# A macaron block on one core: attention probabilities turned by a transposing DMA in place of TensorE transposes

## What is computed

```
x = x + 0.5 * ffn(layernorm(x), router_weight, w_in, w_out, bias)
x = x + attn(layernorm(x), w_q, w_k, w_v, w_o, b_o)
x = x + 0.5 * ffn(layernorm(x), router_weight, w_in, w_out, bias)
# attn: 16 heads of 16; softmax(mask(q k^T) / sqrt(256)) v, then w_o and b_o
# ffn: 8 experts, the best 2 of each token, silu(a) * b, hidden size 512
```

## Time and profile before

| what | value |
|---|---|
| median of 3 runs | 430.71 us (430.55 to 431.05) |
| the profiled execution | 430.32 us, of which the span is 428.6 us |
| TensorE busy | 402.1 us |
| VectorE, ScalarE, GpSimd busy | 299.3, 257.1, 249.2 us |
| mean granted clock of TensorE | 0.975 of 2.4 GHz |
| first mixture layer, attention, close, second layer | about 0 to 153, to 281, to 304, to 428.6 us |

### The profile page before, as it was taken

How to read it: one execution, slowest core, us unless ns; L and a number is a source line. 1 busy time by engine, 2 the same in 40 slices (tenths; PEclk the granted TensorE clock), 3 DMA queues, 4 the chain that set the end, 5 groups by cost and what they waited for, 6 DMA issues and landing times.

```text
span 428.6 us, 10138 instructions
## 1 busy us (share of the span) xinstructions
PE 402.1 (94%) x2892; PEld 331.2 (77%) x2893; DVE 299.3 (70%) x612; ACT 257.1 (60%) x640; POOL 249.2 (58%) x312
## 2 busy tenths in 40 slices
PE   7779999999999989799999999888899999999996
PEld 3558888888888767588888888674588888888884
DVE  6878997756655895877677676967356775566566
ACT  2737866565556455788788787722365555655552
POOL 5355457765478169577777677200555596654860
PEclk9889999999999999999999999966999999999999
DMA  7959911211111800000000000007641212112136
GB/s 253 400 143 397 363 55 40 66 44 61 55 46 38 271 32 2 1 3 3 2 0 0 0 0 0 2 1 254 208 153 50 61 40 66 57 49 55 43 99 219
DMA packets 22059, 38.90 MB, mean 91 GB/s; under 512 B 3217, under 2 KB 14737, under 8 KB 21777
## 3 DMA queue, kind: packets, MB, share of 16 engines
q1 hardware_dynamic: 17168, 24.41, 16.6%
q0 software_dynamic: 4576, 12.07, 9.4%
q10 hardware_dynamic: 288, 2.10, 1.3%
HBM read 29.37 MB, written 9.19 MB: 90 GB/s over the span
## 4 chain that ended last, share of the span: by engine, by line
PE 64%; DVE 15%; DMA 8%; issue 5%; ACT 3%; POOL 3%; ACTq 0%; SPq 0%; DVEq 0%; POOLq 0%
PE bank L1379 25%; PE bank L1401 12%; PE bank L1549 6%; PE bank L1389 4%; PE bank L1560 4%; DMA w_out<-y_scratch 3%; PE bank L1516 3%; PE bank L1355 2%; DMA unused_rows<-in_wr_t,own_row 2%; DMA arena<-xn_scratch,gather_row 1%; DVE arena L902 1%; DMA y_scratch<-arena,scatter_row 1%; DVE pT_lo L1185 1%; DVE v L1255 1%; PE bank L1550 1%
## 5 line engine op out<-in xcount | busy, mean ns | idle before, releaser
L533 POOL DMA_INDIRECT arena<-xn_scratch,gather_row x46 | 51.4, 1117 | 60.8 <-PE bank L1355 39.5
L539 POOL DMA_INDIRECT y_scratch<-arena,scatter_row x42 | 61.1, 1454 | 34.8 <-ACT arena L707 32.0
L1043 DVE TENSOR_TENSOR wo_lo<-w_out,wo_hi 128x1024 fp32r<-128x1024 f32 x46 | 61.2, 1330 | 4.1 <-PE bank L1401 2.5
L1379 PE MATMUL bank<-w_hi,xT_hi 128*128 x184 | 62.4, 421 | 0.0
L1048 DVE TENSOR_TENSOR gT_lo<-bank,gT_hi 128x512 fp32r<-128x512 f32 x46 | 31.7, 689 | 38.7 <-ACT gT_hi L681 38.7
L1379 PE MATMUL bank<-w_hi,xT_lo 128*128 x184 | 57.7, 394 | 0.0
L1379 PE MATMUL bank<-w_lo,xT_hi 128*128 x184 | 57.3, 392 | 0.0
L674 ACT ACTIVATE arena<-bank 128x512 f32<-128x512 f32 x46 | 27.5, 598 | 46.7 <-PE bank L1379 46.7
L619 POOL TENSOR_TENSOR k_head<-k_hi,head_mask 128x256 fp32r<-128x256 f32 x64 | 38.7, 625 | 28.1 <-PE bank L1550 21.0
L696 ACT ACTIVATE wo_hi<-w_out 128x1024 fp32r x46 | 48.8, 1061 | 5.5 <-issue 3.4
L1032 DVE TENSOR_TENSOR xT_lo<-bank,xT_hi 128x256 fp32r<-128x256 f32 x46 | 19.5, 424 | 35.8 <-ACT xT_hi L666 35.6
(11 more groups left out here) (197 smaller groups left out, 961.5 us busy)
## 6 DMA issues: line engine op xcount, KB each, us to landing
w_raw<-in_win_t SPq DMA_DIRECT2D x8, 1024.0 KB, 9.7
w_out<-in_wout_t SPq DMA_DIRECT2D x16, 512.0 KB, 7.8
w_out<-y_scratch SPq DMA_DIRECT2D x8, 512.0 KB, 6.2
xn_scratch<-arena ACTq DMA_DIRECT2D x2, 1024.0 KB, 6.0
x<-in_x SPq DMA_DIRECT2D x4, 256.0 KB, 3.7
out<-x SPq DMA_DIRECT2D x4, 256.0 KB, 2.1
arena<-xn_scratch,gather_row POOLq DMA_INDIRECT x46, 3.5
y_scratch<-arena,scatter_row POOLq DMA_INDIRECT x46, 3.0
```

The costliest lines, as they stand in the source:

```text
L533: pool.indirect_dma_start(out=xb[j % 2][:, :], out_offset=None, in_=xn_dram, in_offset=bass.IndirectOffsetOnAxis(ap=gather_row[:, j:j + 1] ...
L539: pool.indirect_dma_start(out=y_dram, in_=y[j % 2][:, :], in_offset=None, out_offset=bass.IndirectOffsetOnAxis(ap=scatter_row[:, j:j + 1], ...
L1043: dve.tensor_tensor(wo_lo[:, :, :], w_out[:, bass.ds(e, 1), :, :].rearrange("p o c d -> p (o c) d"), wo_hi[u][:, :, :].bitcast(F32), ALU.s ...
L1379: last = pe.matmul(bank[2 * half + u][:, :], tok[u][:, k, :], wts[:, bass.ds(e, 1), k, half * H:(half + 1) * H], start=(part == 0 and k == ...
```

## The change

Exponentials are written back in place, into the bank of the scores. `high` and `low` now come before the turn: they split these banks into `parts`, a f16 buffer of 2 x 6 x 128 columns per parity, in one instruction for the tail tiles (512 columns) and one for the head tiles (256). SP issues one transposing DMA per pair, `parts` to `pT` (32 in all); `weigh` reads `pT` and waits for the DMA. TensorE's `turn_probs` is gone. Head scores alternate between banks 2 and 3. The drain's and the close's warming matmuls, the place of the expert scores in `finish`, and the order on VectorE there change as well. The half bias is now added by VectorE, in four instructions per layer behind blocks 5 and 6. The rehearsal is gone; VectorE's first split of weights waits until GpSimd has issued the first gather.

```diff
-VBANK = (6, 4, 5, 3, 5, 6, 5, 6)
+VBANK = (3, 4, 5, 6, 5, 6, 5, 6)
-WARM_START, WARM_RANKS, WARM_PLAN, WARM_TURNED = 12, ((6, 5), (6, 5)), (6, 6), (4, 4)
-WARM_END, WARM_TURN2, WARM_CHOSEN = 2, 2, 2
+WARM_START, WARM_RANKS, WARM_PLAN, WARM_TURNED = 12, ((6, 5), (6, 5)), (10, 8), (4, 4)
+WARM_END = 6
-WARM_LN = (5, 1, 0, 0)
+WARM_LN = (5, 2, 1, 0)
+WARM_LAST = (4, 4)
+WARM_FINISH = (3, 2, 1)
...
+            def turn_parts(g):
+                u = g % 2
+                sp.wait_ge(low_ready, g * 2 + 2)
+                if g > 1:
+                    sp.wait_ge(pv_done, g * 2 - 2)
+                sp.dma_start(pT[u][:, :, :], parts[u][:, :, :, :].rearrange("p a t k -> p (a t k)"), transpose=True)\
+                    .then_inc(pT_ready[u], 16)
+
             for f in range(2):
                 if f:
+                    for g in range(BATCH * HPAIRS):
+                        turn_parts(g)
...
-            rehearse()
...
-                if f == 0:
-                    pool.wait_ge(rehearsed, 16)
...
                 for j in range(AHEAD):
                     gather(f, j)
+                    if f == 0 and j == 0:
+                        pool.sem_inc(first_begun)
...
-                    reach(act, probsT_done, g * 2 - 2)
                     for hh in range(2):
                         h = 2 * p + hh
-                        act.activation(probs[u][:, hh, 1:3, :],
-                                       bank[u][:, hh * SEQ:(hh + 1) * SEQ].rearrange("p (k t) -> p k t", k=2), ACT.Exp,
-                                       bias=neg_max[u][:, 1, hh:hh + 1],
+                        keys = bank[u][:, hh * SEQ:(hh + 1) * SEQ]
+                        act.activation(keys, keys, ACT.Exp, bias=neg_max[u][:, 1, hh:hh + 1],
...
             def high(b, s):
                 g = b * HPAIRS + (s - SLAG - 1)
-                for hh in range(2):
-                    act.wait_ge(probsT_done, g * 2 + (hh + 1))
-                    reach(act, pv_done, g * 2 + (hh - 3))
-                    act.activation(pT_hi[(s - 1) % 2 * 2 + hh][:, :, :],
-                                   bank[3 + hh][:, 0:3 * P].rearrange("p (k t) -> p k t", k=3),
-                                   ACT.Copy, scale=P_SCALE).then_inc(pT_hi_ready, 1)
+                u = (s - 1) % 2
+                reach(act, pT_ready[u], b * (16 * HPAIRS // 2) + (s - SLAG - 1) // 2 * 16)
+                act.wait_ge(tail_probs_ready, g * 2 + 2)
+                act.activation(parts[u][:, 0, 0:4, :], bank[u][:, :].rearrange("p (t k) -> p t k", t=4), ACT.Copy,
+                               scale=P_SCALE).then_inc(high_ready, 1)
...
+            def add_half_bias(f, i):
+                dve.wait_ge(bias_loaded, 32)
+                dve.wait_ge(xn_ready, TILES * 2 * f + 2 * i + 2)
+                two = x[:, 2 * i:2 * i + 2, :]
+                dve.scalar_tensor_tensor(two, bc(bias_row[:, :], 1, [P, 2, D]), 0.5, two, ALU.mult, ALU.add)\
+                    .then_inc(bias_added, 1)
...
                 if f == 0:
+                    dve.wait_ge(first_begun, 1)
                     split_low(0)
...
+            def low(b, s, tail):
+                g = b * HPAIRS + (s - SLAG - 1)
+                u = (s - 1) % 2
+                tiles = slice(0, 4) if tail else slice(4, 6)
+                source = bank[u][:, :] if tail else bank[2 + u][:, 0:2 * P]
+                dve.wait_ge(high_ready, g * 2 + (1 if tail else 2))
+                dve.scalar_tensor_tensor(parts[u][:, 1, tiles, :], source.rearrange("p (t k) -> p t k", k=P), P_SCALE,
+                                         parts[u][:, 0, tiles, :], ALU.mult, ALU.subtract).then_inc(low_ready, 1)
...
-                    reach(pe, tail_probs_ready, g * 2 - 2)
+                    reach(pe, low_ready, g * 2 - 3)
...
-                    reach(pe, head_probs_ready, g * 2)
-                    to = bank[2][:, 0:2 * P].rearrange("p (h k) -> p h k", h=2)
+                    reach(pe, low_ready, g * 2 - 2)
+                    to = bank[2 + u][:, 0:2 * P].rearrange("p (h k) -> p h k", h=2)
...
             def weigh(b, s):
+                turned = pT[(s - 1) % 2]
+                pe.wait_ge(pT_ready[(s - 1) % 2], b * (16 * HPAIRS // 2) + ((s - SLAG - 3) // 2 + 1) * 16)
...
                 turn_half(0)
-                score_experts(1, (1,))
+                warm(WARM_FINISH[0])
                 turn_half(1)
                 project_half(0)
                 project_half(1)
                 turn(2, (2,))
-                warm(WARM_TURN2)
+                score_experts(1, (1,))
```

More of the change, by code:

```diff
@@ L332, in build @@
         tail_probs_ready = sem("tail_probs_ready")
-        probsT_done = sem("probsT_done")
-        pT_hi_ready = sem("pT_hi_ready")
-        pT_lo_ready = sem("pT_lo_ready")
+        high_ready = sem("high_ready")
+        low_ready = sem("low_ready")
+        pT_ready = [sem(f"pT_ready{u}") for u in range(2)]
         pv_done = sem("pv_done")
@@ L585, in ffn @@
                     scatter(f, j)
[L586 to L591 removed]
+                    if j == SCATTERED // 2:
                         gather_gates(f)
@@ L831, in step @@
                                        scale=1.0 / P_SCALE).then_inc(ctxT_ready, 1)
+                    if old if s < SLAG + 1 else new:
+                        high(b, s)
                     if old if s < SLAG else new:
@@ L856, in step @@
                                     .then_inc(v_second_ready, 1)
-                    if old if s < SLAG + 1 else new:
-                        high(b, s)
             def finish():
@@ L1135, in body @@
                         weigh_slots(f)
+                        add_half_bias(f, 0)
+                    if isinstance(j, int) and j == PEELED - 1:
+                        for i in range(1, TPAIRS):
+                            add_half_bias(f, i)
                 for j in range(PEELED):
@@ L1224, in step @@
                         maxima(b, s, True)
-                    if s in CHUNK_STEP and (old if s < SLAG + 2 else new):
-                        low(b, s)
+                    if old if s < SLAG + 1 else new:
+                        low(b, s, True)
                     if old if s < SLAG else new:
@@ L1230, in step @@
                         chunk(b, CHUNK_STEP.index(s))
-                    if s not in CHUNK_STEP and (old if s < SLAG + 2 else new):
-                        low(b, s)
+                    if old if s < SLAG + 1 else new:
+                        low(b, s, False)
                     if not new and s == 0:
@@ L1551, in scores @@
                     .then_inc(tail_scored if tail else head_scored, 1)
-            def turn_probs(b, s):
-                g = b * HPAIRS + (s - SLAG - 2)
-                for hh in range(2):
-                    pe.wait_ge(head_probs_ready, g * 2 + (hh + 1))
-                    reach(pe, pT_lo_ready, g * 2 + (hh - 1))
-                    for i in range(3):
-                        last = pe.transpose(bank[3 + hh][:, i * P:(i + 1) * P], probs[s % 2][:, hh, i, :], ident[:, :])
-                    last.then_inc(probsT_done, 1)
             def weigh(b, s):
@@ L1605, in step @@
                         scores(b, s, True)
-                    if old if s < SLAG + 2 else new:
-                        if not old and s == SLAG + 2:
-                            pe.wait_ge(v_rest_ready, VALUES[SLAG][1])
-                        turn_probs(b, s)
-                        if not new and s >= SLAG:
-                            pe.wait_ge(attn_added, BATCH)
-                            warm(WARM_END, 7)
+                    if not new and s >= SLAG:
+                        pe.wait_ge(attn_added, BATCH)
+                        warm(WARM_END, 7)
                     if not new and s == SUM_STEP - 1:
@@ L1620, in step @@
                         chunk(b, CHUNK_STEP.index(s))
+                    if not old and s == SLAG + 1:
+                        pe.wait_ge(v_rest_ready, 1)
                     if old if s < SLAG else new:
```

58 lines of the change are left out of this document (21 added, 37 removed).

## The result

The changed kernel takes **433.89 us** (median of 21 runs, 429.9 to 435.8), the kernel before 430.62 beside it (21 runs, 427.6 to 433.9): ratio **1.0067**, 95% interval 1.0045 to 1.009. It is slower by 1.9 to 3.9 us, where 6.5 less was forecast. The profiled execution took 432.4 us, its span is 430.4.

The account below looks back on a forecast made before the run. TensorE, busy 94%, was taken as the bound, not by much. Loop batches -5.1, first batch -0.7, drain +1.3, close -1.5, bias -0.5, start 0: -6.5 from 430.3 gives 423.8 us; range 414 to 437.

Parts of the forecast that it names:

- Part 1, the transposes: Attention loop: transposes leave TensorE, 5.5 us a batch, its floor falling from 27.4 to 21.9; copies and subtractions cost the same.
- Part 2, the landing time L: Attention: time for each pair's 384 KB transposing DMA to land, taken as 4.4 us, bounds 2.35 and 7.3.
- two steps take at least 1.5 + L: Attention: parts buffer's ring of tail copy, head copy, head subtraction, hand-overs and L; 2.95 us a plain step.
- one-bank ring of 2.65: Attention plain step: tail scores, maximum, then the tail subtraction that frees their bank for two pairs on; about 2.65 us.
- hidden wholly: Rival, chance 0.20: attention's transfer lands in under 3.8 us, a batch takes 24.7, the kernel about 420.
- The zero-gain point, L = 5.2: Attention: landing time at which five plain steps take 3.34 us each and a batch stays at 27.4.
- the transfer is the bound: Rival, chance 0.22: above L = 5.2 the parts-buffer ring sets every attention step; 437 us at 5.8, about 460 at 7.3.
- the clock falls in attention: Rival, chance 0.05: 1.2 GHz granted in attention, TensorE's batch nearly doubles to 43, +15.6 us a batch, near 475.
- each block as its own transfer: Rival, chance 0.03: attention's twelve blocks each pay 1.6 us, 19 us a pair, +500 us, about 930.
- Part 3, the drain: After the attention loop: the last pair's landing replaces transpose and copy, partly under warming matmuls and row scaling; +1.3 us.
- Part 4, the close: Behind the drain: scoring of pair 1 leaves the path, warming matmuls may hold the clock; -1.5 us, bounds 0 and -3.
- Part 5, the bias: Mixture layers: GpSimd's addition and TensorE's 0.73 us stall go, VectorE gets four operations a layer; -0.5, bounds -0.7 and +1.

Follow-up runs that it names:

- e2_order: Changed kernel with VectorE's head subtraction moved directly behind its tail subtraction, ahead of head maximum and chunk: 424.97 us, ratio 0.986 to the kernel before.
- e13_ahead_chunk: Changed kernel with the head subtraction ahead of the head maximum only in the two chunk steps of a batch: ratio 0.9903 to the kernel before.
- e14_ahead_plain: Changed kernel with the head subtraction ahead only in the six steps without a chunk: ratio 1.0063 to the kernel before.
- e7_order_two: Changed kernel with the head subtraction ahead and each pair's transfer split into high and low parts: ratio 0.9963 to the kernel before.
- e1_close: Kernel before with only the change's warming matmuls and order in drain and close: ratio 0.9972 to the kernel before.
- e6_half: Changed kernel transferring only the six high-part blocks, still behind the head subtraction, low parts left out of the result: ratio 0.9774 to the kernel before.
- e11_order_held: Changed kernel with the head subtraction ahead and three warming matmuls in four plain steps of a loop batch: 424.25 us, ratio 0.9835 to the kernel before.
- e8_order_late: Changed kernel with the head subtraction ahead and a one-block transfer, waited for, in front of each transfer: ratio 1.0772 to the kernel before.

## Why the prediction was wrong

- **Part 1, the transposes** (5.5 us a batch off TensorE): right. Copies and subtractions cost what was written, 0.61 and 0.70 for the tail. TensorE's busy time falls by only 11.6 us in all, because 5.0 more go into warming and the same chunks (20.2 us for 16.7), scores (63.7 for 61.3) and weighings (59.8 for 56.3) are busy longer.
- **Part 2, the landing time L**: 3.7 us, inside the bounds of 2.35 and 7.3 and under the 4.4 taken. The estimate from the Trainium skill, DMA: Bandwidth & Descriptors, gave 3.5, and the trace agrees better with it than with mine; the fixed 2.0 us in it stand there for transfers issued by GpSimd, and these are issued by SP, so how much of the agreement is luck stays open.
- **Part 2, "two steps take at least 1.5 + L"**: here it failed. I followed the parts buffer from the landing to its own next landing and added the copies and the head subtraction, as if the head subtraction ran as soon as its copy was there. The diff has it last on VectorE in the step, behind the head maximum, which waits for head scores, which in two of eight steps wait for a chunk. That ring takes three steps and 10.15 us where mine has two and 3.9 + 1.5. As a lower bound the formula was not broken; the error was to take it for what sets the step. The runs e2_order, e13_ahead_chunk and e14_ahead_plain show it: with the chunk out of the ring a batch takes 25.4 to 25.6 us, with it in, 27.4 or more.
- **The 25.7 a batch and the 423.8 us** are not confirmed by the version with the line moved, though it comes near them (25.4 to 25.6, and 424.97 and 424.62 us). They were made with L = 4.4; with the measured 3.7 my formula gives 2.6 a step, under the one-bank ring of 2.65, and a shorter transfer did not help there (e7_order_two). The nearness in the total is luck in part too: the bias gave 1.3 us more than forecast, and the attention less.
- **Rival "hidden wholly"** (0.20): this is the miss in full. Its condition, L under 3.8, was met, and it promised 24.7 a batch and about 420 us; the kernel took 27.4 or more and 433.89. A shorter L than the forecast was to be worth 4 us more, and was worth nothing, since the ring that counted was not in the sum.
- **The zero-gain point, L = 5.2**: followed from the same formula; the real one was at or just below the L that was there (27.4 to 28.0 us a batch at 3.7, 25.5 at 2.8).
- **Rival "the transfer is the bound"** (0.22): its mechanism was right, its condition (L above 5.2) wrong. **Rival "the clock falls in attention"** (0.05): it did, in patches of 4 to 8 us, not throughout; 3 us in a batch, where 15.6 was priced. Of the signs of being wrong this is the one that came; the tail copies waited 0.4 us a step (10.1 us in 24 steps), under the 0.5 that was named. Its counter-evidence, a first batch at 22.7 of 27 us busy with a full clock, did not carry over.
- **Rival "each block as its own transfer"** (0.03): no. One block takes 2.6 us, six take 2.8, twelve 3.7 (medians); a further block costs far less than a transfer of its own.
- **Part 3, the drain** (+1.3): the two traces have the drain at 20.7 and 20.4, but the first has a low clock in it (0.65 from 280 to 284). At a full clock the order before takes 19.6 (e1_close, with the new warming in it) and the change 20.4, so about +0.8, nearer to the forecast than the table is. The transfer is not wholly covered there: halved, it gives 19.4 (e6_half). All these are single executions.
- **Part 4, the close** (-1.5): measured alone -1.2 (-2.4 to 0). Right, for warming and order together; which of the two it was is not told apart.
- **Part 5, the bias** (-0.5, not under -0.7): measured alone -1.8 (-2.8 to -0.8). The mechanism is there (the stall of 0.73 gone, no other in its place), but the stall alone is less than the interval's near end. In the second layer the trace before has a `wo_lo` of 2.93 us beside the addition at 344.18, and no stall of TensorE; what else GpSimd's two additions cost stays open.
- **Part 6, the start** (0): nothing to be told by putting the old start back. Right.
- **The sum**: close and bias alone give -3.0. If they add up in the change as they do alone, attention costs +5.9 by the first measurement of the change and +3.2 by the second, where -4.5 was forecast. The range, 414 to 437, held the time; the direction was wrong.

The version that comes out of it, the change with the head subtraction ahead, takes 424.97 and 424.62 us in two measurements, **1.4% less than before** (ratios 0.986 and 0.9857) and better than both kernels. What sets its 25.4 us a batch stays open: not TensorE's work (e11_order_held), not the transfer's size (e7_order_two). Its longest waits, VectorE for the tail scores (12.8 us) and TensorE for a subtraction (6.4), are like those of the prediction's ring through one bank; that this ring sets the batch is likely and not shown.

## What to carry to other kernels

When a transfer replaces an engine's work, its landing time is one term of a ring, and the others are what stands ahead of its **trigger** and behind its **landing** in each engine's order, whatever they belong to. Walk the ring instruction by instruction in program order, through special steps too, until it comes back to the same instruction, and divide by the steps passed. Then put the trigger ahead of everything that waits for others, unless its supplier waits for that.

## What was not expected of the hardware

A transposing transfer from SBUF to SBUF takes at least 2.2 us for one block of 128 x 128 halves (median 2.6, e8_order_late), 2.7 for six (2.8, e6_half) and 3.7 for twelve (3.7, the change): 0.1 to 0.17 us a further block by the shortest times. The granted clock fell towards 0.50 in the change each time right behind 4 us in which TensorE had been busy 1.60, 2.89 and 2.62 us (176 to 180, 192 to 196, 248 to 252); but in the kernel of e2_order 2.98 of 4 (200 to 204) were followed by 1.00, and in the kernel before 2.84 (180 to 184). What decides it is not settled by these rows. It is worth 3 us in one batch of the change. Single traces mislead by such amounts: the close seemed worth 3.5 and was worth 1.2.
